# A recurrence step whose first digit of h is one multiplication with a float16 result, on the 2h x 2^-14 scale

## The reference, cut to what matters

```
xt = swapaxes(x, 0, 1)                    # 3136 = 56*56 tokens, one after the other
xi, xg, xo = xt@U_i + b_i, xt@U_c + b_c, xt@U_o + b_o
def step((h, c), ...):
    i = sigmoid(xi_t + h@V_i); g = tanh(xg_t + h@V_c); o = sigmoid(xo_t + h@V_o)
    c_new = h*c + i*g
    h_new = o*tanh(c_new)
```

## Time and profile before

| | us |
|---|---|
| median of 3 runs | 4079.02 (4078.55 to 4084.59) |
| the profiled execution, its time | 4080.13 |
| the profiled execution, its span | 4078.4 |
| rows without recurrence, to the first gate activation | 199.13 |
| the 3136 steps, to the last step's end | 4074.2 - 199.1 = 3875.0 |

### The profile page before, as it was taken

The page is one execution under the profiler, slowest core; times in us unless marked ns, Lnnn a source line. Parts: engine busy times, 40 slices in busy tenths (PEclk is TensorE's granted clock), DMA queues, the critical chain, the costliest instruction groups (busy, mean ns, idle before and its releaser), DMA issues.

```text
span 4078.4 us, 134734 instructions
## 1 busy us (share of the span) xinstructions
PE 3620.0 (89%) x35548; PEld 2656.5 (65%) x35548; DVE 3425.5 (84%) x21828; ACT 2635.9 (65%) x11666; POOL 2154.5 (53%) x3173
## 2 busy tenths in 40 slices
PE   6799998989898989899999999898989898988887
PEld 5666666666666666666666666666666666666665
DVE  6788888888888888888888888888888888887777
ACT  3366666666666666666666666666666666666665
POOL 6555555555555556555555555555555555652222
PEclk8855555555555555555555555555555555555555
DMA  5000000000000000000000000000000000000000
GB/s 73 2 1 1 1 1 1 1 1 1 1 1 1 1 1 1 1 1 1 1 1 1 1 1 1 1 1 1 1 1 1 1 1 1 1 2 1 1 1 1
DMA packets 44538, 11.08 MB, mean 3 GB/s; under 512 B 39913, under 2 KB 44010, under 8 KB 44490
## 3 DMA queue, kind: packets, MB, share of 16 engines
q1 hardware_dynamic: 42378, 10.05, 1.7%
q10 hardware_dynamic: 2112, 0.46, 0.1%
HBM read 7.29 MB, written 3.21 MB: 3 GB/s over the span
## 4 chain that ended last, share of the span: by engine, by line
PE 57%; ACT 18%; DVE 18%; issue 6%; POOL 1%; DMA 0%; ACTq 0%; DVEq 0%; POOLq 0%
PE GATES L1267 12%; ACT O L698 10%; PE GATES L1284 9%; PE YB L1087 9%; ACT G L695 8%; DVE HR L917 8%; DVE O L914 8%; PE TAPB L1074 6%; PE YB L1238 6%; PE DB L1206 5%; PE DB L1068 3%; PE H1B L1114 1%; PE H2B L1114 1%; PE H2B L1062 1%; PE TAPB L1121 1%
## 5 line engine op out<-in xcount | busy, mean ns | idle before, releaser
L695 ACT ACTIVATE G<-GATES 128x12 f32<-128x12 f32 x3136 | 573.4, 183 | 1197.8 <-PE GATES L1284 1149.3
L1267 PE MATMUL GATES<-HR,VN 128*128 128x4 f16 x3136 | 536.3, 171 | 357.5 <-DVE HR L917 239.3
L1284 PEld LDWEIGHTS GATES<-HR,VN 128*128 128x128 f16 x6272 | 423.0, 107 | 657.7 <-issue 593.4
L909 DVE TENSOR_TENSOR_SCAN CT<-G,CT 128x12 f32<-128x12 f32 x3136 | 586.7, 187 | 272.1 <-ACT G L695 250.6
L698 ACT ACTIVATE O<-G 128x16 f32<-128x16 f32 x3136 | 690.5, 220 | 99.2 <-ACT G L695 0.2
L914 DVE RECIPROCAL O<-O 128x4 f32<-128x4 f32 x3136 | 567.6, 181 | 198.7 <-ACT O L698 1.0
L1280 PEld LDWEIGHTS <-VN 128*128 128x128 f16 x3136 | 457.6, 146 | 345.8 <-issue 309.5
L917 DVE TENSOR_TENSOR_SCAN HR<-O,CT 128x20 f16<-128x20 f32 x3136 | 613.4, 196 | 5.2
L1284 PE MATMUL GATES<-HR,VN 128*128 128x4 f16 x6272 | 617.1, 169 | 0.0
L1284 PE MATMUL GATES<-H,VW 128*128 128x4 f16 x6272 | 615.7, 169 | 0.0
L926 DVE SCALAR_TENSOR_TENSOR CT<-HIST,CT 128x4 f32<-128x4 f32 x3136 | 523.7, 167 | 108.8
(11 more groups left out here) (242 smaller groups left out, 7023.1 us busy)
## 6 DMA issues: line engine op xcount, KB each, us to landing
out_dram<-OUT SPq DMA_DIRECT2D x112, 28.0 KB, 2.0
X<-in_x_dram SPq DMA_DIRECT2D x4, 672.0 KB, 11.5
STG<-in_L_ffn_w_dram SPq DMA_DIRECT2D x4, 512.0 KB, 12.6
U<-in_L_conv_U2s_dram SPq DMA_DIRECT2D x1, 972.0 KB
W<-in_L_ffn_w_dram SPq DMA_DIRECT2D x1, 512.0 KB, 11.9
X<-in_x_dram ACTq DMA_DIRECT2D x4, 112.0 KB, 3.1
S<-in_L_conv_S1s_dram SPq DMA_DIRECT2D x1, 108.0 KB
S<-in_L_conv_S2s_dram SPq DMA_DIRECT2D x1, 108.0 KB
```

Source lines behind the costliest of these rows:

```text
L695: act.activation(G6[:, :, 2:5], gates[c][:, w, :, :], ACT.Tanh, scale=1 / GSCALE).then_inc(step_in, 1)
L909: dve.tensor_tensor_scan(CELL.rearrange("z b k -> z (b k)"), G6[:, :, :].rearrange("z b k -> z (b k)")[:, 0::2], ADD3.rearrange("z b k -> ...
L1267: return pe.add_instruction(mybir.InstMatmult(name=nc.get_next_instruction_name(), engine=mybir.EngineType.PE, start_tensor_calc=False, st ...
L1284: last = pe.matmul(gates[c][:, w, :, SLOT[g]], wt[:, g].rearrange("z m c -> z (m c)"), digit, start=False, stop=True, skip_group_check=True)
```

## The change

It replaces line 917's scan by a tensor_tensor multiplication of 4 elements (output gate x tanh of the cell) whose float16 result is rounded by the conversion: h is kept as 2h x 2^-14, below the smallest normal float16 numbers, where float16's numbers have one spacing. `HR` shrinks to one value per batch element. `O5` keeps one copy per batch element, of 6 elements instead of 2 x 5: the added one (1/HSCALE) scales the second digit up. So line 921's scan runs over 24 elements instead of 20, and line 698 writes 8 values instead of 16. The digits' weights are `VW` for the first and `VB` = VW x 2^-14 for the second. Gates, inputs and weights are rescaled by powers of two. No instruction moves to another place on any engine; one memset of 4 columns is added in the first rows.

```diff
-GSCALE, WSCALE = 1024.0, 64.0
+GSCALE, WSCALE, XSCALE = 0.5, 64.0, 2.0 ** -3
-GRID = 1.5 * 2.0 ** 13
+HSCALE = 2.0 ** -14
+GRID = 0.75
...
-        O5 = sb("O5", [128, 2, B, 5])
-        HR = sb("HR", [128, B, 5], F16)
-        H5 = sb("H5", [128, B, 5], F16)
+        O5 = sb("O5", [128, B, 6])
+        HR = sb("HR", [128, B], F16)
+        H5 = sb("H5", [128, B, 6], F16)
...
-        TC5 = CT[:, 32:52].rearrange("z (b k) -> z b k", k=5)
+        TC5 = CT[:, 32:56].rearrange("z (b k) -> z b k", k=6)
...
-                act.activation(X4S[:, :], X4D[:, :], ACT.Copy).then_inc(x4_done, 1)
+                act.activation(X4S[:, :], X4D[:, :], ACT.Copy, scale=XSCALE).then_inc(x4_done, 1)
...
-                    act.activation(O5[:, :, :, 1:5:3], G6[:, :, 3:4].unsqueeze(1).broadcast_to([128, 2, B, 2]), ACT.Copy, scale=O_MAX, bias=1.0)\
+                    act.activation(O5[:, :, 1:5:3], G6[:, :, 3:4].broadcast_to([128, B, 2]), ACT.Copy, scale=O_MAX * HSCALE, bias=HSCALE)\
...
-                    dve.reciprocal(O5[:, 1, :, 3], O5[:, 1, :, 1]).then_inc(rec_done, 1)
+                    dve.reciprocal(O5[:, :, 3], O5[:, :, 1]).then_inc(rec_done, 1)
                     dve.wait_ge(t_done, 1 + n + 1)
-                    dve.tensor_tensor_scan(HR[:, :, :].rearrange("z b k -> z (b k)"), O5[:, 0].rearrange("z b k -> z (b k)"),
-                                           TC5.rearrange("z b k -> z (b k)"), 0.0, op0=ALU.mult, op1=ALU.add)\
-                        .then_inc(hd1_done, 1)
+                    dve.tensor_tensor(HR[:, :], O5[:, :, 1], TC5[:, :, 0], ALU.mult).then_inc(hd1_done, 1)
                     dve.wait_ge(rec_done, 1 + n + 1)
-                    dve.tensor_tensor_scan(H5[:, :, :].rearrange("z b k -> z (b k)"), O5[:, 1].rearrange("z b k -> z (b k)"),
+                    dve.tensor_tensor_scan(H5[:, :, :].rearrange("z b k -> z (b k)"), O5[:, :, :].rearrange("z b k -> z (b k)"),
...
-                        link(dve, dve.memset(O5[:, :, :, 2:3], -1.0))
+                        link(dve, dve.memset(O5[:, :, 2:3], -1.0))
+                        link(dve, dve.memset(O5[:, :, 5:6], 1.0 / HSCALE))
...
-                    for done, wt, digit in ((hd1_done, VN, HR[:, :, 2]), (hd2_done, VW, H5[:, :, 4])):
+                    for done, wt, digit in ((hd1_done, VW, HR[:, :]), (hd2_done, VB, H5[:, :, 5])):
```

More of the change, by code:

```diff
@@ L192, in build_program @@
         VW = sb("VW", [128, 3, 2, C], F16)
-        VN = sb("VN", [128, 3, 2, C], F16)
+        VB = sb("VB", [128, 3, 2, C], F16)
         ONE = sb("ONE", [1, TOK])
@@ L736, in act_head_row @@
                     act.wait_ge(rec_lo, 6)
-                    act.activation(VN[:, :, :, :], VW[:, :, :, :], ACT.Copy, scale=-1.0).then_inc(rec_set, 1)
+                    act.activation(VB[:, :, :, :], VW[:, :, :, :], ACT.Copy, scale=HSCALE).then_inc(rec_set, 1)
         @block.scalar
@@ L967, in dve_head_row @@
                         if part == 0:
-                            last = dve.scalar_tensor_tensor(out=UX[:, 1, g, m, :], in0=UF[:, g, :], scalar=a,
+                            last = dve.scalar_tensor_tensor(out=UX[:, 1, g, m, :], in0=UF[:, g, :], scalar=a / XSCALE,
                                                             in1=UX[:, 0, g, m, :], op0=ALU.mult, op1=ALU.subtract)
@@ L973, in dve_head_row @@
                         else:
-                            last = dve.scalar_tensor_tensor(out=VW[64:128, g, m, :], in0=VF[64:128, g, :], scalar=0.5 * a,
+                            last = dve.scalar_tensor_tensor(out=VW[64:128, g, m, :], in0=VF[64:128, g, :], scalar=0.5 / HSCALE * a,
                                                             in1=VH[64:128, g, :], op0=ALU.mult, op1=ALU.subtract)
@@ L1035, in _ @@
             dve.tensor_copy(GBB[:, :, :], TAPB[0:TOK, 300:300 + 2 * E].rearrange("z (p e) -> z p e", p=2))
-            link(dve, dve.memset(CT[:, 0:52], 0.0))
+            link(dve, dve.memset(CT[:, 0:56], 0.0))
             link(dve, dve.memset(ADD3[:, :, 0:2], 1.0))
```

12 lines of the change are left out of this document (6 added, 6 removed).

## The result

The changed kernel takes 4057.47 us (median of 4 runs, 4055.54 to 4059.07), the kernel before on the same chip 4080.03 us (4078.55 to 4084.59). The ratio is 0.9943, interval 0.993 to 0.9956: 22.6 us less, where the prediction had 63 us less. The sign and the range held, the size did not. The time is the one that the prediction gave to rival A (4058).

The account below looks back on a forecast made before the run. The chain of dependences inside each of 3136 steps was taken as the bound. A 35 ns gain per step, less places giving it back, made 54.3 us (50 full rows) plus 8.8 (last 6), 63.1: 4080.1 to 4017, range 3986 to 4060.

Parts of the forecast that it names:

- rival A: HR's hold on H shrinks only by its elements: H starts at 96 ns, 22 us gained, 4058; chance 0.12.
- the sum for the end of the chain: From HR's start to the second digit's product: H's start 73, its length 175, 53 to the product; 301 ns.
- g: Gain per step at the end of the chain behind HR's start: 336 - 301 = 35 ns.
- HR as a multiplication: First digit's instruction: HIST's 133 plus 25 behind a wait, 158 ns instead of 196; digit ready 38 ns earlier.
- When H may start: H behind HR: 158 less 85 lying under the next instruction, 73 ns; bounds 50 and 96.
- H with 24 elements: Second digit's scan: at 1.1 ns an element, 171 + 4 = 175 ns.
- The products 0.09 apart: TensorE's first and second digit's products were to stay 0.09 us apart.
- Where g is given back: Fills tied to the cell's tanh (SI, PA): eleven places a row lose 35 ns each; total 1802 x g, 63.1 us.
- B: Nothing given back at SI and PA fills, or more DVE overlap: 110 us gained, 3970; chance 0.12.
- signs of being wrong: H starting at 0.11 or later, the named places not lengthening, or TensorE late where it now has slack.
- C: Slower: a scan can't overlap the multiplication ahead, H starts at 158 ns, 90 us added, 4170; chance 0.05.
- D: No difference: float16 results or products in this range cost the saving, or something unseen binds; 4080 within 8; chance 0.04.

Follow-up runs that it names:

- histfirst: Changed kernel with the HIST multiplication moved ahead of HR's: 4232.36 us (kernel before on that chip 4075.76).
- scan20: Changed kernel with HR made by a scan of 20 elements over one repeated value, H at 24: 4096.84 us (kernel before 4082.39).
- multonly: Kernel before with only HR's scan replaced by the multiplication of 4 elements, H over 20: 4045.21 us (kernel before 4075.76).
- scan12: Changed kernel with HR made by a scan of 12 elements over one repeated value, H at 24: 4070.08 us (kernel before 4082.39).
- h20: Changed kernel with H's scan stopped after 20 of its 24 elements: 4046.56 us (kernel before 4073.95).
- twocopy: Changed kernel with two copies of O5, HR and HIST reading one, H the other: 4056.71 us (kernel before 4075.76).

## Why the prediction was wrong, point by point

The step that failed is the sum for the end of the chain, "73 + 175 + 53 = 301 ns". It carried H's recorded length over from behind a scan of 20 (171, plus 4) to behind a multiplication of 4, where H lasts 196. The end came at 325 ns: 21 of the missing 24 ns are in H's length, 3 in its start. So g was 10 to 11 ns and not 35; what each ns was worth in the whole kernel was forecast about rightly (1.8 us, measured 2.0).

**HR as a multiplication: right, its reason only in part.** 158 ns forecast, 159 measured, and the first digit comes 37 ns earlier. The 25 ns that the forecast added were put down to the wait. Of them 8 are the wait's: a multiplication of 4 lasts 159 behind a wait and 151 behind a multiplication (histfirst), a scan of 20 lasts 196 and 188 (scan20, multonly). The other 17 to 18 are the record that is shorter behind a scan (171 and 133). Both rows that the forecast used, HIST's 133 and H's 171, stand behind a scan, so the sum came out. By the same split H over 20 elements is 171 + 17 = 188 behind a multiplication, as multonly has it. A float16 result costs what a float32 result costs (histfirst).

**When H may start: right as a number, wrong as a term.** 73 ns forecast, 76 measured. (The 73 came from 158 less 85 that lie under the next scan; measured, 83 lie under it.) But the sum took H's start and H's length for two independent terms. They aren't: behind a scan of 20 the same H starts late by 36 ns and is short by 17 (multonly against before). What failed is its argument "what counts is not HR's duration but how long it holds back the next instruction", read from recorded starts. What counts is when H ends, and that moves by some 1.04 ns for each element ahead. The value for that stood in the prediction as the upper bound and as rival A, "if only the 16 elements go": 16 elements, 16 to 18 ns.

**H with 24 elements: wrong.** 175 forecast, 196 measured; 17 of the missing 21 ns are the shared start just named, 4 are the slope. The 1.1 ns an element came from two scans with different operands, the cell scan (12 elements, 187) and HR (20, 196). The same form at 12 lasts 179 (scan12), and the slope is 2.06. Two shapes that differ in more than their size gave a slope that was none.

**The sum.** Forecast 73 + 175 + 53 = 301 ns behind HR's start, measured 76 + 196 + 53 = 325, from 336 (335 by the medians): g was to be 35, and is 10 to 11. By the parts: 18 ns won by 16 elements fewer ahead (multonly), 8 lost by 4 elements more in H (h20).

**The products 0.09 apart: wrong.** They are 0.11 apart, since H has stayed behind while the first digit came early. Of the first digit's 37 ns, 26 go into that greater distance and win nothing.

The Trainium skill's figure ("Vector Engine (DVE) Microarchitecture Reference", section "Measured stream behaviour on trn2"), 75 ns per instruction and 1.04 ns a column, agrees with the runs on two counts: 76 ns hold behind 4 elements (by it 79), and 1.04 per element of whatever stands ahead, scan or multiplication. It doesn't hold for a scan's own time, 2.06 ns an element. An estimate that takes it for both instructions, 16 x 1.04 less 4 x 1.04, would be 12.5 ns, nearer than mine. It was in the prediction as 79 ns for H's start, in the same sum that let H's length be.

**O, HIST, weights: right.** O at 213 has no effect, nor has 224 (twocopy); HIST lasts 133 as before. h20 and multonly, which differ in all of these parts, have stages of 3840.7 and 3840.8 us.

**Where g is given back: right.** The medians of the places in the full rows, before and after, in ns:

| place | before | after |
|---|---|---|
| ordinary (most of the 56 lie within 3 of it) | 1225 | 1214 |
| 14, 19, 24 (SI and convolution) | 1229, 1225, 1224 | 1239, 1232, 1233 |
| 29, 34, 39 (the same) | 1226, 1226, 1225 | 1233, 1232, 1232 |
| 26, 31, 36, 41, 46 (PA and expert product) | 1282, 1271, 1269, 1276, 1273 | 1293, 1286, 1285, 1286, 1285 |
| 21 (PA, one wait) | 1225 | 1213 |
| 10, 2 (TensorE late by itself) | 1303, 1255 | 1305, 1258 |

Places 0, 6 and 8 are long as well (1339, 1247, 1282 before) and gained 10, 18 and 11. The eleven named places got longer, by 8 ns (SI) and 13 (PA) on average, no other of the 56 did by more than 3; SI's end to DB stayed 56 and 55 ns, PA's end to the taps 129 to 136 and 128 to 135. That the fills are tied to the tanh shows directly: counted from the second digit's product ahead of it, PA ended after 80 ns and now ends after 92 (at place 21: 79 and 91), SI after 172 and now 184, later by g. Place 21, which was to gain nothing of 35, gained the full 11: with so small a g its slack was enough. In h20, where the ordinary step gained 18, it gained 4 (1221), so the slack does run out as forecast. Summed over all 56 places of a row the medians fell by 378 ns, 50 rows 18.9 us; of the last six rows I take 48 x (-11) + 46 = -482 ns each, 2.9 us (the medians over their places sum to -478). Together 21.8 us, and 21.5 was measured. The prediction's weight 1802 with g = 11 gives 19.8; with nothing given back, 3136 x 11 ns would be 34.5 us.

**The rivals.** A was what happened, in its mechanism (only the elements count) and nearly in its time (4058 against 4057.5), though not in its start of 96. That its g of 12 fits so well is in part luck: it has 16 ns for the elements ahead and takes off 4 for those in H, where 18 and 8 were measured. I had held line 926 against it, which is followed after 0.07. That was right of H's start, 76, and misled because the start is not what counts. B is out, the eleven places show the giving back. What the prediction names as signs of being wrong, a start of H at 0.11 or later, places that don't lengthen, TensorE late elsewhere, did not come: none of them looked at H's length. C is out, H starts 76 ns into an instruction of 159. D is out by the interval.

## What to carry to other kernels

Two instructions back to back on the vector engine, of which the second ends the chain, are to be priced by the end of the second, not by its start: shrinking the first by 16 elements was worth 18 ns, though its own record lost 37. A recorded length holds only behind the kind of instruction that it was read behind. Take a slope only from rows that differ in nothing but the size. Ask of every win in a recurrence which fills are tied to an event inside it; here a second wait on TensorE, put ahead of five such fills, was worth nearly as much as the whole change (16 to 18 us, against 21.5).

## What the runs showed of the hardware that I had not expected

- A scan takes 2.06 ns an element (163, 179, 196 for 4, 12, 20), a multiplication 1.03 (159, 175, 196 for 4, 20, 40); but either delays the end of the next instruction by about 1.04 for each of its elements only. Behind a scan the next record starts later and is shorter by 1 ns an element.
- One more 4-element instruction ahead of H costs 69 ns (histfirst), although it lasts 151 to 159.
- The first instruction behind a wait lasts only 8 ns longer than the same one behind a multiplication: 159 and 151 for the multiplication of 4 (histfirst), 196 and 188 for the scan of 20 (scan20, multonly).
- Two waits ahead of one TensorE product make it start 128 to 135 ns behind the event, one wait 55. With the wait that ends last put second it was 93 to 105 (102 to 109 in the kernel before); moving the other wait to the engine that signals the first brought all of it back, 73 ns in each of the five steps.
- The small scale of h costs nothing, neither in the vector engine's float16 result nor in TensorE's products: HR lasts 159 ns in multonly, where h has its old scale, and in after; the digits' products last 176 and 168 ns in multonly, 175 and 168 in after. On this scale the first digit is below the smallest normal float16 number when h is below 0.5 in size, and up to twice that number otherwise; what share of the values lay below, no run recorded.
